# Attention scores computed twice, the second time with (head, key) pairs on the partitions

## The reference

```
q = layernorm(x) . Wq,  k = ctx . Wk,  v = ctx . Wv          per head, 8 x 8 matrices
p = softmax(where(mask == 0, -1e20, q k^T) / sqrt(8))        16 heads x 128 x 77
x = x + tanh(g_x) * (concat(p v) . Wo^T + bo)
h = layernorm(layernorm(x)) * gamma + beta
x = x + tanh(g_f) * (shared expert(h) + top_prob * expert[argmax(router(h))](h))
```

## Time and profile before

| | |
|---|---|
| median of 3 runs | 823.26 us (818.33 to 832.54) |
| profiled execution | 821.43 us, its span 819.6 us |
| mean granted TensorE clock | 0.915 of 2.4 GHz |

### The profile page before, as it was taken

How to read it: one execution, slowest core, us unless ns; L and a number is a source line. 1 busy time by engine, 2 the same in 40 slices (tenths; PEclk the granted TensorE clock), 3 DMA queues, 4 the chain that set the end, 5 groups by cost and what they waited for, 6 DMA issues and landing times.

```text
span 819.6 us, 20037 instructions
## 1 busy us (share of the span) xinstructions
PE 627.8 (77%) x6457; PEld 477.4 (58%) x6458; DVE 573.2 (70%) x1634; ACT 395.3 (48%) x1024; POOL 524.4 (64%) x865
## 2 busy tenths in 40 slices
PE   0479999999999999999999999820030088888884
PEld 0147677677777677667777777610020077877773
DVE  4647888878888888877877887659930067776762
ACT  1045566556556556556646645422122065555651
POOL 5046767767777777776876876517977425555554
PEclk9989999999999999999999999955565589999997
DMA  9300000000000000000000000001111122222220
GB/s 240 105 1 9 2 10 9 2 10 10 2 10 10 4 6 10 9 2 8 10 2 10 10 2 2 2 1 53 50 50 53 43 51 67 58 62 65 62 60 17
DMA packets 32966, 24.39 MB, mean 30 GB/s; under 512 B 5138, under 2 KB 30302, under 8 KB 32880
## 3 DMA queue, kind: packets, MB, share of 16 engines
q1 hardware_dynamic: 25088, 12.20, 5.9%
q0 software_dynamic: 4352, 8.53, 3.1%
q10 hardware_dynamic: 3440, 2.55, 1.2%
HBM read 14.13 MB, written 9.65 MB: 29 GB/s over the span
## 4 chain that ended last, share of the span: by engine, by line
PE 55%; issue 15%; DVE 15%; SPq 6%; DMA 5%; ACT 1%; POOL 1%; another core or an unknown queue 0%; POOLq 0%; DVEq 0%; ACTq 0%
PE PS L1069 13%; PE PS L1080 9%; PE PS L1043 7%; PE PS L1059 5%; PE PS L1053 3%; PE PS L1037 3%; PE PS L1091 2%; DMA X<-in_x 2%; DMA out<-res,tin 2%; DVE stq L558 2%; SPq L260 2%; PE PS L1111 2%; PE PS L1252 2%; DVE mx L512 2%; DMA tin<-rows 2%
## 5 line engine op out<-in xcount | busy, mean ns | idle before, releaser
L1069 PE MATMUL PS<-ident,prob 128*77 128x128 f32 x1024 | 138.8, 279 | 0.9 <-ACT hq L827 0.6
L1069 PEld LDWEIGHTS PS<-ident,prob 128*77 128x77 f32 x1024 | 114.4, 148 | 14.1 <-issue 11.8
L846 ACT COPY shared<-PS 77x512 f32<-77x512 f32 x128 | 74.4, 582 | 85.1 <-PE PS L1069 85.0
L864 ACT ACTIVATE prob<-PS 128x616 f32<-128x616 f32 x128 | 87.5, 684 | 52.4 <-PE PS L1059 49.6
L357 POOL TENSOR_TENSOR part<-prob 128x624 f32<-128x624 f32 x64 | 96.8, 1512 | 18.0 <-ACT prob L864 18.0
L512 DVE TENSOR_REDUCE mx<-PS 128x8 f32<-128x616 f32 x128 | 101.0, 789 | 9.0 <-PE PS L1043 8.3
L438 POOL DMA_INDIRECT out<-res,tin x72 | 73.9, 1027 | 30.1 <-issue 29.8
L334 POOL TENSOR_TENSOR vm<-ctxq,ones 77x128 f32<-77x128 f32 x64 | 29.1, 454 | 93.0 <-PE PS L1080 93.0
L524 DVE COPY shared<-PS 77x512 f32<-77x512 f32 x128 | 87.0, 680 | 2.1 <-PE PS L1069 1.9
L426 POOL DMA_INDIRECT rows<-prob,pay_i x64 | 72.6, 1134 | 17.2 <-issue 15.7
L1080 PE MATMUL PS<-shared,vm 77*32 77x128 f32 x2048 | 82.0, 279 | 0.2 <-DVE X L544 0.2
(11 more groups left out here) (219 smaller groups left out, 1554.7 us busy)
## 6 DMA issues: line engine op xcount, KB each, us to landing
tin<-rows SPq DMA_DIRECT2D x72, 66.0 KB
X<-in_x SPq DMA_DIRECT2D x8, 512.0 KB, 9.9
ctxq<-in_ctx SPq DMA_DIRECT2D x16, 154.0 KB
out<-res,tin POOLq DMA_INDIRECT x72
w2n<-in_ew ACTq DMA_DIRECT2D x1, 1024.0 KB, 11.0
rows<-prob,pay_i POOLq DMA_INDIRECT x64
rows<-padding SPq DMA_DIRECT2D x9, 66.0 KB
w1n<-in_sw ACTq DMA_DIRECT2D x1, 128.0 KB, 11.9
```

Source lines behind the costliest of these rows:

```text
L846: nc.scalar.copy(PT[:, s, 2 * u, :], PS[0:SK, 4, :]).then_inc(pt_copied[0], 1)
L864: nc.scalar.activation(prob[:, s, u, :, :, 0:SK], PS[:, 2 * u:2 * u + 2, 0:GK].rearrange("p g (i k) -> p g i k", k=SK), ACT.Exp, scale=flo ...
L1069: ins = nc.tensor.transpose(PS[0:SK, 4 + v, i * P:(i + 1) * P], prob[:, s, u, v, i, 0:SK], ident[:])
```

## The change

The scores are made in two layouts. The first, with queries on the partitions, serves only the maximum: one plain fp32 product per group instead of three fp32r products. The second has the (head, key) pairs of a group on the partitions: 4 x 78 = 312 pairs in three chunks of 104 (a 78th, empty key for each head), queries in the columns. The maxima of all 16 heads, split by GpSimd in three bf16 parts (`split_max`), are transposed by one product (`transpose_max`) and lie with the mask in a bf16 operand `moving` (48 rows of maxima, 77 of mask); twelve bf16 products with a table of ones and zeros, `pairsel`, add mask and maxima to the second scores (`shift`). The exponentials of these are already what weighing needs, so nothing of the probabilities is transposed or copied. The row sums come from TensorE: a second stationary operand `own` (ones where a pair belongs to a head) goes through the same probabilities as the values; VectorE takes the reciprocal of the sums, 128 x 128, and multiplies. The bias goes in through a bf16 product (`onesb`, `bo3`) in `project`.

The context is loaded twice: as before for the keys (`ctxp`, single buffer, one transfer for four elements) and in six pieces into the layout of the pairs (`ctxq`). GpSimd's root for the router now includes the variance's scaling, in two parts over two steps; VectorE aggregates statistics for every element. `keep_busy` is gone. Loops are written out flat, and the pipeline is one step deeper: step t has the scores of t, the shift of t - 1, the weighing of t - 2, the projection of t - 3. The transposes for x, context, keys and h use bank 6 as before, in `misc`, at the end of a step; both halves of the first scores use banks 0 and 1, the second scores banks 2 to 5.

The diff, cut to its core:

```diff
@@ transfers (SP)
+                for i in range(GH):
+                    row, end = i * SP, i * SP + SK
+                    while row < end:
+                        c = row // CR
+                        stop = min(end, (c + 1) * CR)
+                        k = row - i * SP
+                        sp.dma_start(ctxq[row - c * CR:stop - c * CR, s, :, c, :],
+                                     A["ctx"][bass.ds(q * QB, QB), k:k + stop - row].rearrange("b k d -> k b d")).then_inc(ctx_in[s], 16)
...
@@ GpSimd
+            def split_max(b):
+                pool.wait_ge(max_ready, 2 * b + 2)
+                ge(pool, nmT_psum, b)
+                nc.gpsimd.tensor_copy(nm3[:, 0:H], nm[:, b % 2]).then_inc(split_step, 1)
...
+                nc.gpsimd.tensor_tensor(nm3[:, 2 * H:3 * H], nm_rest[:], nm3[:, H:2 * H], ALU.subtract).then_inc(nm_split, 1)
@@ VectorE
+            def normalise(b):
                 dve.wait_ge(pv_done, b + 1)
+                nc.vector.reciprocal(rinv[:], PS[:, 7, P:2 * P]).then_inc(rinv_done, 1)
+                dve.wait_ge(rinv_done, b + 1)
+                ge(dve, proj_done, b)
+                nc.vector.tensor_tensor(oT[:], PS[:, 7, 0:P], rinv[:], ALU.mult).then_inc(o_ready, 1)
@@ ScalarE
+            def copy_max(b):
+                act.wait_ge(nmT_psum, b + 1)
+                ge(act, shifted, 2 * b)
+                nc.scalar.copy(moving[0:PARTS * H, :], PS[0:PARTS * H, 6, 0:P]).then_inc(moving_ready, 1)
+            def exps(b, u):
+                act.wait_ge(shifted, 2 * b + u + 1)
                 ge(act, pv_done, b - 1)
+                nc.scalar.activation(PT[:, b % 2, 2 * u:2 * u + 2, :], PS[0:CR, 2 + 2 * u:4 + 2 * u, 0:CH * P], ACT.Exp,
                                      scale=float(1.0 / np.sqrt(HD))).then_inc(exp_done, 1)
@@ TensorE
-            keep_busy(9)
-            keep_busy(6)
+            def scores(b, u):
+                q, j = b // QB, b % QB
+                ge(pe, max_ready, 2 * b + u)
+                for v in range(2):
+                    nc.tensor.matmul(PS[:, v, 0:GK], identb[:], maskneg[:].rearrange("p i k -> p (i k)"),
                                      start=True, stop=False)
...
+                for v in range(2):
+                    g = 2 * u + v
+                    r = slice(g * GR, (g + 1) * GR)
+                    ins = nc.tensor.matmul(PS[:, v, 0:GK].rearrange("p (i k) -> p i k", k=SK), xT[r, q % 2, j * P:(j + 1) * P],
+                                           kbd[r, q % 2, j, :, 0:SK], start=False, stop=True, tile_position=(g * GR, 0))
+                ins.then_inc(scores_ready, 1)
+            def transpose_max(b):
+                pe.wait_ge(nm_split, b + 1)
+                misc_free(b)
+                nc.tensor.matmul(PS[0:PARTS * H, 6, 0:P], nm3[:], identb[:], start=True, stop=True).then_inc(nmT_psum, 1)
+            def scores_of_pairs(b):
+                q, j = b // QB, b % QB
+                ge(pe, exp_done, 2 * b)
+                for c in range(CH):
+                    for g in range(G):
+                        r = slice(g * GR, (g + 1) * GR)
+                        nc.tensor.matmul(PS[0:CR, 2 + g, c * P:(c + 1) * P],
+                                         kbd[r, q % 2, j].rearrange("p i k -> p (i k)")[:, c * CR:(c + 1) * CR],
+                                         xT[r, q % 2, j * P:(j + 1) * P], start=c == 0, stop=False,
+                                         tile_position=(g * GR, 0), skip_group_check=True)
+            def shift(b):
+                pe.wait_ge(moving_ready, b + 1)
...
+                for u in range(2):
                     for g in (2 * u, 2 * u + 1):
+                        for c in range(CH):
+                            ins = nc.tensor.matmul(PS[0:CR, 2 + g, c * P:(c + 1) * P],
+                                                   pairsel[:, g].rearrange("p i k -> p (i k)")[:, c * CR:(c + 1) * CR],
+                                                   moving[:], start=False, stop=c == CH - 1, skip_group_check=True)
+                    ins.then_inc(shifted, 1)
+            def weigh(b):
+                pe.wait_ge(exp_done, 2 * b + 2)
+                ge(pe, o_ready, b)
+                for w, col in ((own[:], P), (vm[:, b % 2], 0)):
...
+                    for c in range(CH):
+                        for g in range(G):
+                            ins = nc.tensor.matmul(PS[g * GR:(g + 1) * GR, 7, col:col + P], w[:, c, :] if col else w[:, c, g, :],
+                                                   PT[:, b % 2, g, c * P:(c + 1) * P], start=c == 0, stop=c == CH - 1,
+                                                   tile_position=(0, g * GR))
+                ins.then_inc(pv_done, 1)
             def project(b, logits_of=None):
...
+                nc.tensor.matmul(PS[:, 7, 2 * P:2 * P + D], oT[:], WVO[:], start=True, stop=False)
+                ins = nc.tensor.matmul(PS[:, 7, 2 * P:2 * P + D], onesb[:], bo3[:], start=False, stop=True)
...
+            for t in range(B + 3):
+                if t < B:
+                    scores(t, 0)
+                if 1 <= t < B + 1:
+                    transpose_max(t - 1)
+                    scores_of_pairs(t - 1)
+                    shift(t - 1)
+                if t < B:
+                    scores(t, 1)
+                if t >= 3:
+                    project(t - 3, t // QB - 3 if t % QB == 2 and 3 <= t // QB < NQ else None)
+                if 2 <= t < B + 2:
+                    weigh(t - 2)
+                if t < B:
+                    misc(t)
```

More of the change, by code:

```diff
@@ new lines, in _ @@
+            for b in range(QB):
+                expand_keys(b)
+            for b in range(B):
+                q, j = b // QB, b % QB
+                if b >= 1:
+                    make_vm(b - 1)
+                if j >= 1 and q + 1 < NQ:
+                    expand_keys(b + QB - 1)
+                if j == 0 and q >= 1:
+                    expand_keys(b + QB - 1)
+                if j < 2 and q >= 2:
+                    root(q - 2, j)
+                split_max(b)
+            make_vm(B - 1)
@@ L412, in carry @@
+            for q in (NQ - 2, NQ - 1):
+                root(q, 0)
+                root(q, 1)
             def carry(n):
@@ L526, in sums @@
[L526 to L532 removed]
+                ge(dve, nm_split, b - 1)
@@ L618, in route @@
+            for t in range(B + 4):
+                if t < B:
+                    take_max(t, 0)
+                if t % QB == 3 and 3 <= t // QB < NQ:
+                    dve.wait_ge(proj_done, t - 3)
+                    keep_logits(t // QB - 3)
+                if t >= 4:
+                    residual(t - 4)
+                    aggregate(t - 4)
+                if t < B:
+                    take_max(t, 1)
+                if 2 <= t < B + 2:
+                    normalise(t - 2)
             def route(part_):
@@ L904, in _ @@
[L904 to L916 removed]
+            make_xn(0, 0)
+            make_xn(0, 1)
+            act.wait_ge(maskT_psum, 1)
@@ new lines, in _ @@
+            nc.scalar.copy(moving[:], PS[:, 5, 0:P]).then_inc(maskT_copied, 1)
+            act.wait_ge(maskT_copied, 1)
+            copy_xT(0)
+            copy_ctxT(0)
+            copy_kp(0)
+            copy_ctxT(1)
+            for t in range(B + 1):
+                q, j = t // QB, t % QB
+                if t >= 1:
+                    copy_max(t - 1)
+                    exps(t - 1, 0)
+                    exps(t - 1, 1)
+                if t == B:
+                    break
+                if j < 2 and q + 1 < NQ:
+                    make_xn(q + 1, j)
+                if j >= 2 and q >= 2:
+                    make_h(q - 2, j - 2)
+                if j == 0 and q + 1 < NQ:
+                    copy_kp(q + 1)
+                if j == 1 and q + 1 < NQ:
+                    copy_xT(q + 1)
+                if j == 2 and q + 2 < NQ:
+                    copy_ctxT(q + 2)
+                if j == 3 and q >= 2:
+                    copy_h(q - 2)
@@ L918, in fill_pay @@
+            for q in (NQ - 2, NQ - 1):
+                make_h(q, 0)
+                make_h(q, 1)
+                copy_h(q)
             def fill_pay(q, s):
@@ L993, in _ @@
         def _(pe):
-            def keep_busy(n):
-                for _ in range(n):
-                    nc.tensor.matmul(PS[:, 5, :], onesb[:], onesb[:].unsqueeze(1).broadcast_to([P, BANK // P, P]),
-                                     start=True, stop=True)
             pe.wait_ge(bd_ready, 1)
@@ L1086, in spread_sums, with transpose_x @@
-            def spread_sums(b, s, maxima):
-                pe.wait_ge(rinv_done, b + 1)
-                ge(pe, mt_copied, maxima)
-                ge(pe, spread_copied, b)
-                nc.tensor.matmul(PS[:, 6, P:2 * P], rinv[:, s].rearrange("p h d -> p (h d)"), ident[:],
-                                 start=True, stop=True).then_inc(spread_psum, 1)
+            def transpose_x(q):
+                pe.wait_ge(xn_ready, q + 1)
+                for j in range(QB):
```

(2 more changed lines are left out.)

654 lines of the change are left out of this document (221 added, 433 removed).

## The result

The kernel after takes **750.43 us** (median of 4 runs, 748.01 to 751.73) where the kernel before took 821.18 beside it (4 runs, 818.33 to 832.54): a ratio of 0.9146, 95% interval 0.9099 to 0.9192; the ratio leaves out the run of 832.54 us, which is over 1.5% above the fastest of its kernel. The profiled execution took 750.47 us, its span is 748.5 and its mean granted clock 0.915, as before.

The account below looks back on a forecast made before the run. TensorE's instruction stream was taken to bound the attention stage. Terms of -0.46 and waits of -0.13 cut the step from 7.48 to 6.89 us; over 64 steps, 821.4 - 38 + 2 = 785 us, range 754 to 815.

Parts of the forecast that it names:

- the shift: Twelve bf16 products with 104-column stationary operands: between 0.70 and 1.10 us a step on TensorE; 1.10 taken, +0.43 net.
- the slow line: Load times of 32 and 77 four-byte columns, 109 and 148 ns: 0.87 ns more a column, 0.09 us for 104.
- The quick-load rival: In the shift, loads are quick and it costs 0.70 us, 0.40 less a step: 759 us; chance 22%.
- The forecast step: One step of TensorE's stream in the attention stage falls from 7.48 to 6.89 us.
- weighing: 24 products in four column groups, including those for the sums: 1.41 us for 1.15, +0.26 a step.
- projection: A bf16 product adds the bias, and the projection now stands between two changes of tiling: +0.25 us a step.
- The waits: TensorE's waits for the maxima on VectorE, 6.9 us in 400 us, get a longer cover: -0.13 us a step.
- no other engine comes near: VectorE 6.1 us a step at most, ScalarE no longer than now, GpSimd little over half: none near TensorE's 6.9.
- TensorE could not be fed: At 20 ns an instruction, weighing and pair scores starve TensorE: +0.6 us a step, 823 us; chance 14%.
- Row groups that do not overlap: Fp32 products in row groups slow both scores: +1.3 us a step, 868 us; with no overlap 977 us; chance 11%.
- A late small copy: The moving copy or the split comes late and costs 0.2 us a step: 798 us; chance 6%.
- The ends: Start and drain around the steps, warming products gone, perhaps a colder start: together +2 us, between -4 and +7.

Follow-up runs that it names:

- Experiment 2: Kernel after plus, in every step, 12 products of 8 columns with changing stationary operands of several widths, bf16 and fp32, to price loads: 928.13 us.
- Experiment 3: Kernel after with twelve more products of the shift's form ahead of the pair scores in every step, their result overwritten: 800.84 us.
- experiment 4: Kernel after with the 12 fp32 products of the scores by pairs made twice in every step: 791.28 us.
- experiment 5: Kernel before with the eight transposes of probabilities of the first half of every step issued twice: 855.87 us.
- experiments 8 and 9: Kernel after with first scores from bf16 copies: 711.59 us; then that kernel with ScalarE's bf16 copy of x made from SBUF, not PSUM: 700.93 us.
- experiment 10: The 700.93 us kernel (bf16 first scores, second copy from SBUF) with the transposes and key projection issued ahead of the weighing: 722.14 us.
- experiment 6: Kernel after with 9 and 6 warming products of 512 bf16 columns put back between the first products of weights: 750.5 us.

## Why the prediction was wrong

**The step that failed** is the shift: "the term that the trace does not show", taken at its upper bound of 1.10 us because "every load of less than 128 columns is on the slow line". It took 0.71 us, the lower bound. 0.39 x 64 = 25 us of the 34.5 between 785 and the profiled 750.47. The slow line was drawn from four-byte loads, and the fp32 products of the earlier trace rows, and applied to two-byte ones. Experiment 2 shows both halves of the error: a bf16 load of 104 columns is slower than a full one, as argued, but takes 48 ns where an fp32 one of 104 takes 92, and so stays below the 56 ns of columns that hide it. Experiment 3 has the columns' pace again, 56 ns, in twelve more products of the form. (The prediction reads 0.11 us a load from eight in 0.81, which is 0.10, and by it the upper bound would have been about 1.0 us; within a group the probe has 0.112, so this is not what failed.) The question was never whether the load is quick but whether it is longer than what streams above it. The quick-load rival named the right time for the step (0.70) with a reason that does not hold for 104 columns.

**The terms that held.** The forecast step, 6.89 us, less the 0.39 is 6.50; measured 6.49. Each of the others is within 0.06: scores (1.07 for 1.07), maxima, scores by pairs (0.85 for 0.84, doubled in experiment 4: +0.66), weighing, projection. Eight transposes in before cost 0.87 (experiment 5; priced at 0.88 and a change of tiling). The waits went as said; by experiment 5 they were 0.20 us a step and not 0.13, so a few hundredths in other terms cancel against it. That no other engine comes near was right with room to spare: VectorE 55, ScalarE 49, GpSimd 42 of 100 us, although the reciprocal of 128 columns takes 0.96 us of VectorE.

**The rivals.** TensorE could not be fed: false, 100.00 of 100 us busy. Row groups that do not overlap: false. A late small copy: no wait in the trace of after, but experiments 8 and 9 found one as soon as the step became shorter, at the copies that must leave the shared bank 6 and not at the copy of the maxima or the split that the prediction watched; in experiment 10 it was the inputs of the moved work.

**The ends and the range.** The ends were put at +2. The stage's own ends cost +2.3 (61.7 us gained for 64 in steps) and its later start +0.9; the colder start that was named as possible is there. In after the same 24 instructions take 1.62 and then 0.92 us:

```profile
64.75 1.62 PE L983 MATMUL PS<-xT,kbd 32*104 32x128 f32 x24
66.30 1.52 PE L996 MATMUL PS<-moving,pairsel 128*104 128x128 bf16 x12
...
72.06 0.92 PE L983 MATMUL PS<-xT,kbd 32*104 32x128 f32 x24
72.91 0.88 PE L996 MATMUL PS<-moving,pairsel 128*104 128x128 bf16 x12
```

The clock column of this trace reads 1.00 in both places; 1.62 us is what the same products take at a granted 0.50 in experiment 6 (from 56.58 us on). The other 10.6 us, with the opposite sign, are the routing and expert stages of one execution of before that were longer than in every other one. The sum was made against that one profile (821.4 us) and the range held nothing for it. With the shift at 0.71 the sum would have been 760; it is those 10.6 us that then still part it from the time, and that the lower end of 754 had no room for.

## What to carry to other kernels

Before an upper bound for a hidden operation goes into a sum, ask whether it is longer than what hides it: compare the load with the columns that stream above it, and take its price from rows of the same element size. Where TensorE is busy all the time its step can be summed from start-to-start distances, here to 0.05 us a term, and they also show waits that the view of idle time leaves out. The stages around it took some 10 us more in one profiled execution than in the others, and the sum started from that one: such a spread belongs into the range. Here the next wait, after the step became shorter, was for copies out of a PSUM bank that two kinds of work share; moving the work earlier helped only together with what produces its inputs, and the idle time ahead of ScalarE's exponentials had room for those.

## What the runs showed of the hardware

- Distance between products of 8 columns, each with a load of its own, by the records of the probe: in bf16 25 ns for loads of 128 columns, 48 for 104, 32 for 64, 25 for 32; in fp32, an instruction, 112 ns for 128, 92 for 104, 58 for 64. From 64 to 104 columns a bf16 load grows by 0.4 ns a column and an fp32 one by 0.85. Of the partial bf16 loads those of 64 and 104 columns are slower than the full one.
- Twelve bf16 products of 128 columns with twelve different loads of 104 start 56 ns apart (experiment 3, both dozens). A change between tile shapes behind them costs 0.09 us.
- In the probe the granted clock fell in the middle of a stage in which TensorE was busy all the time. Stretches of the probe, clock in the third column from the end:

```profile
100.00:200.00 100.00, 100.00 (x1458) 73.63 (x1451) 41.97 (x86) 35.15 (x68) 33.31 (x102) 0.88 0.09 26
300.00:400.00 100.00, 100.00 (x1252) 73.16 (x1243) 36.78 (x76) 31.47 (x61) 27.81 (x84) 0.74 0.06 18
```

  The only difference to after, with 1.00 in all of them, is the probe's products of 8 columns. The first fall, at 95.1 us, came right behind the first fp32 group of them (92.27 to 95.00); the four bf16 groups between 66 and 86 us saw none. The falls are part of why its 928 us are more than its products add, and why paces were read where the clock was 1.00.
- Fifteen products of 512 columns ahead of the stage did not shorten the stretch at 1.2 GHz behind them in the one execution traced (to 80 us; in after products are slow up to 68), and the end of that stretch varied between executions of one kernel (at about 59 and 95 us in before). What sets it stays open.
